# Four layers in one Trainium2 kernel: second cross-attention's norm and blocks, the scan's opening, and the order of the head loop in self-attention

## The chip, the cores and the metric

One core of one Trainium2 chip runs the whole program. The metric is the device time of one execution in microseconds; lower is better. Everything is float32. The engines are TensorE (PE in the profile, PEld its weight loads), VectorE (DVE), ScalarE (ACT), GpSimd (POOL) and SyncE (SP), which issues the transfers here. Each engine runs its own instructions in order, and they meet through semaphores.

## The reference

Four layers follow each other on `x` of 8 batches x 512 tokens x 256 features, with a context of 8 x 64 x 192.

```
L0: h = ln(x); x += Wo softmax(q k / sqrt(64)) v     16 heads of 64, 512 keys (self-attention)
    h = ln(x); x += attention(h, context)             16 heads of 64, 64 keys
    h = ln(x); x += (a * gelu(gate)) W2 + b2
L1: p = silu(context pre_w1) pre_w2; h = [p, x]       64 + 512 = 576 tokens in each batch
    4 layers: xz = rmsnorm(h) W_in; xi = silu(conv(x part)); dt, B, C = xi W_x
              state = exp(dt A) * state + dt * B * xi; y = (C . state + D xi) * silu(z); h += y W_out
    h = rmsnorm(h), the first 64 tokens dropped
L2: xn = layernorm(x); q = xn Wq; k, v = layernorm(context) Wkv; 16 heads of 16, 64 keys
    x += softmax(q k / 4) v Wproj + bproj             (second cross-attention)
    x += gelu(layernorm(x) W1 + b1) W2 + b2
L3: x += single-head attention of layernorm(x) over layernorm(context)
```

## The kernel before

`X` holds the activations in SBUF for the whole run, features on the partitions. The stages run one after the other, each in a block with one program for each engine, and a block ends when all its engines have ended: self-attention, first cross-attention, feed-forward, the scan (`mamba`), the last norm of L1, second cross-attention, feed-forward, last attention. All orders are written by hand. Banks 6 and 7 of PSUM are two lanes, `lane_v` (taken over mostly by VectorE) and `lane_s` (by ScalarE), each with a semaphore for full and one for free; events on a lane have a fixed order, so a step on a lane waits until the event before it has been read.

**Self-attention** (`self_attention`). A loop over 8 batches. Projections of q and k come first, 128x512 each. Then 18 iterations h: the program's heads go in 16 steps h, each with two units u. A unit of *scores* (L394) is the product of 128 queries with 512 keys for two heads (j), which go to banks 2u and 2u+1. VectorE takes the negated maximum of both (L456), ScalarE the two exponentials with their sums (L535), VectorE the reciprocal (L462), and GpSimd multiplies (L574). Two iterations later (LAG = 2, g = h - 2) a *turn* of 8 transposes (L385) lays the unit's probabilities out in banks 4 (copied by VectorE, L451) and 5 (by ScalarE, L527). A *mix* (L371) multiplies the values with both turned units of step g - 1, into a lane. Two mixes fill a lane, which VectorE (L470) or ScalarE (L507) copies to `q`. Between the units of every iteration TensorE's order is turn(g, 0), scores(h, 0), mix(g - 1), turn(g, 1), scores(h, 1). In the iterations h = 0 and 1 the values are projected (L339). While a batch runs, the next batch's norm is worked in: mean after g = 3, square after g = 4, variance after g = 9, scaling on VectorE after g = 10 (L480), and four key projections after g = 14. A unit of scores waits for the exponentials of the unit before it in the same banks, a turn for the multiplied probabilities and for the copies of the turn before it, a mix for both copies of its two turns.

**The scan** (`mamba`). 9 chunks of 512 columns in each of 4 layers, 36 bodies in a loop. A body has 32 pairs j: SyncE spreads dt and u over the partitions (`spread_dt`, `spread_u`, 4 transfers each, for 8 pairs) and loads B and C (`load_bc`, 16 transfers of 256 KB, each for one of 8 values a and one half q; `bc_ready[a // 2]` counts them); GpSimd multiplies u with B into a ring of 6 pairs (L2523), ScalarE makes exp(dt A) (L2492), VectorE scans (L2445) and multiplies with C (L2247) or GpSimd does (L2528), TensorE folds each pair into y (L2388) and works in the projections of the chunks ahead. The *opening* ahead of the loop does for the first chunk what the loop does one chunk ahead: norm, projections (L1956, L1974), silu, softplus, `times_x` (L2261, L2264: u = dt * xi for half of the channels and the reset of dt at a batch's begin), the spreads (L2276, L2283) and B and C (L2292). All engines of the opening but VectorE first wait for `set_up`, six small VectorE steps, one of which clears z (L2400, 128x4096). SyncE waits for all four counts of `u_done` ahead of the first spread; the spreads and then all 16 `load_bc` follow. The first matmul of the loop's count `summed` reads z (L2362).

**Second cross-attention** (`cross_attention_2`). 8 batches of 4 tiles (t) of 128 queries; n counts tiles. The keys of a batch lie as a block-diagonal matrix in `kblk`, the values in `vblk`, two buffers each, brought by `bring_blocks` in 8 + 2 transfers on one semaphore (L1199, L1203). For each tile: scores (L1364), VectorE maximum (L1406) and subtraction (L1410), ScalarE exponential (L1467), VectorE row sum (L1415) and reciprocal (L1417) one tile later, GpSimd multiplication (L1292), a turn two tiles later (L1346) and ScalarE's copy (L1479). Around it, per batch: mean of batch b + 2 (L1301, at t = 1), centring on VectorE (L1392, last but the residual in the iteration t = 1), square, variance of batch b + 1 (L1308, at t = 0), scale on GpSimd (L1285, after the multiplication of tile t = 0), the affine step on ScalarE (`affine`, L1442, at t = 2 ahead of the turned copy), queries (L1315, L1319, at t = 3), mix of batch b - 1 (L1326, L1330, at t = 2), and two output projections (L1339) with residuals on VectorE (L1398). Both output projections go over `lane_v`. SyncE brings the blocks of batch b when the mix of batch b - 2 has been read.

## Time and profile before

| | us |
|---|---|
| median of 3 runs | 6905.54 |
| lowest, highest | 6900.05, 6907.67 |
| the profiled execution's own time | 6903.88 |
| its span | 6902.1 |

| engine | busy us | share of the span |
|---|---|---|
| TensorE | 6161.2 | 89% |
| VectorE | 5114.1 | 74% |
| ScalarE | 3778.9 | 55% |
| GpSimd | 4645.8 | 67% |

The granted clock of TensorE is 0.947 of full over the profiled execution. The shares are means over stages with different limits, so each edit is read in its own stage: by the windows of the stages, then by the timeline in them. In a timeline row the first number is the start, the second the time from the start to the end of the group, then engine, line and operation, the operands, the count, and in brackets how long the engine was idle before and what released it. The ends of matmuls are modelled, so the distance from one start to the next is the safer number. A score matmul or a mix matmul of the program stands as two records.

### The profile page before, as it was taken

To read this page: it belongs to the slowest core of one execution; us is meant where nothing else is said; L and a number is where in the kernel's file an instruction comes from. 1 tells how busy PE (TensorE), PEld (TensorE's weight loads), DVE (VectorE), ACT (ScalarE), POOL (GpSimd) and SP (SyncE) were. 2 spreads that over 40 slices of the span, in tenths; PEclk is the share of its full clock that TensorE was granted. 3 is DMA by queue.
4 is the path that set the end of the run, shared out by engine and by line. 5 is a ranking of instruction groups with operands and counts; after the bars stand their busy time and mean duration, and the time that the engine had idled before them with its cause. 6 is when DMAs were issued, how large, how long until landed. Compare 5 with 4: busy or idle time off the path is not lost. (4 is left out here: it accounts for less than half of the span.)

```text
span 6902.1 us, 73695 instructions
## 1 busy us (share of the span) xinstructions
PE 6161.2 (89%) x20586; PEld 2565.1 (37%) x20586; DVE 5114.1 (74%) x5939; ACT 3778.9 (55%) x6915; POOL 4645.8 (67%) x2163
## 2 busy tenths in 40 slices
PE   9999999999998888888888888888888888888898
PEld 4444444544443333223333323333323333323444
DVE  4444444553226999999999999999999999995623
ACT  4444444532225666666666666666666666664432
POOL 3333333323006999999999999999999999993300
PEclk9999999999999999999999999999999999999998
DMA  2000000113003333333332333233333232332000
GB/s 77 0 0 0 0 0 0 63 44 105 12 0 71 74 78 74 77 90 79 73 80 69 80 84 84 68 80 68 80 84 84 68 85 64 86 78 56 5 0 25
DMA packets 228700, 387.51 MB, mean 56 GB/s; under 512 B 46304, under 2 KB 64416, under 8 KB 225936
## 3 DMA queue, kind: packets, MB, share of 16 engines
q1 hardware_dynamic: 228368, 383.75, 22.9%
q8 instruction: 127, 2.08, 0.1%
q14 instruction: 205, 1.68, 0.1%
HBM read 207.14 MB, written 23.40 MB: 33 GB/s over the span
## 5 line engine op out<-in xcount | busy, mean ns | idle before, releaser
L2523 POOL TENSOR_TENSOR work<-work,weights 128x1024 f32<-128x1024 f32 x1152 | 2692.2, 2363 | 24.3 <-DMA weights<-mamba_bc 13.0
L2388 PE MATMUL banks<-work 128*64 128x512 f32 x4608 | 1359.8, 672 | 568.2 <-POOL work L2528 568.0
L2445 DVE TENSOR_TENSOR_SCAN banks<-banks,work 128x512 f32<-128x512 f32 x1368 | 1712.4, 1274 | 39.5 <-ACT banks L2492 39.3
L2492 ACT ACTIVATE banks<-work 128x512 f32<-128x512 f32 x2304 | 1501.1, 680 | 68.6 <-DVE work L2241 43.2
L2445 DVE TENSOR_TENSOR_SCAN work<-banks,work 128x512 f32<-128x512 f32 x936 | 1175.1, 1271 | 109.2 <-ACT banks L2492 71.9
L2528 POOL TENSOR_TENSOR work<-work,weights 128x1024 f32<-128x1024 f32 x468 | 1103.9, 2359 | 159.7 <-ACT work L2118 159.7
L1956 PE MATMUL banks<-work,weights 128*128 128x512 f32 (+31 forms) x3796 | 1141.1, 451 | 3.0 <-DVE work L2214 3.0
L574 POOL TENSOR_TENSOR work<-work 128x1024 f32<-128x1024 f32 x256 | 484.4, 1895 | 802.6 <-DVE work L462 802.6
L2247 DVE TENSOR_TENSOR work<-banks,weights 128x512 f32<-128x512 f32 x1368 | 905.4, 673 | 0.0
L1956 PEld LDWEIGHTS banks<-work,weights 128*128 128x128 f32 x3796 | 634.4, 190 | 601.0 <-issue 523.5
L2388 PEld LDWEIGHTS banks<-work 128*64 128x64 f32 x4608 | 269.0, 144 | 1426.0 <-POOL work L2528 866.1
L2122 ACT ACTIVATE work<-banks 128x2 f32<-128x2 f32 x684 | 117.3, 171 | 1019.6 <-DVE work L2247 1011.2
L456 DVE TENSOR_REDUCE work<-banks 128x2 f32<-128x1024 f32 x256 | 312.3, 1223 | 155.6 <-PE banks L394 155.6
L535 ACT ACTIVATE work<-banks,work 128x512 f32<-128x512 f32 x512 | 346.5, 684 | 77.9 <-DVE work L456 77.9
L1974 PE MATMUL banks<-work,weights 128*128 128x512 f32 x592 | 351.9, 724 | 0.0
L1011 PE MATMUL banks<-work,weights 128*128 128x512 f32 x768 | 341.2, 598 | 9.7 <-ACT work L215 9.7
L451 DVE COPY work<-banks 128x512 f32<-128x512 f32 x256 | 175.2, 684 | 164.9 <-PE banks L385 164.9
L394 PE MATMUL banks<-work 64*128 64x512 f32 x1024 | 284.7, 638 | 5.6 <-ACT work L502 5.6
L385 PE MATMUL banks<-ident,work 128*128 128x128 f32 x2048 | 281.1, 279 | 5.1 <-ACT work L527 4.7
L527 ACT ACTIVATE work<-banks 128x512 f32<-128x512 f32 x256 | 152.8, 597 | 232.3 <-PE banks L385 231.8
L385 PEld LDWEIGHTS banks<-ident,work 128*128 128x128 f32 x2048 | 221.3, 140 | 150.8 <-issue 79.8
L371 PE MATMUL banks<-work 128*64 128x256 f32 x2048 | 249.3, 385 | 14.7 <-DVE work L480 8.4
(317 smaller groups left out, 7355.4 us busy)
## 6 DMA issues: line engine op xcount, KB each, us to landing
weights<-mamba_bc SPq DMA_DIRECT2D x592, 256.0 KB, 5.0
work<-work SPq DMA_DIRECT2D x1160, 128.0 KB, 2.3
weights<-mamba_taps SPq DMA_DIRECT2D x5, 2048.0 KB, 7.4
weights<-cross_vo SPq DMA_DIRECT2D x16, 512.0 KB, 6.9
mamba_taps<-work SPq DMA_DIRECT2D x4, 2048.0 KB, 6.7
cross_vo<-weights SPq DMA_DIRECT2D x6, 1024.0 KB, 9.0
work<-in_conv_rows SPq DMA_DIRECT2D x16, 256.0 KB, 7.1
out_T<-X SPq DMA_DIRECT2D x8, 512.0 KB, 3.3
```

The costliest lines, as they stand in the source:

```text
L385: mm = e.transpose(core.banks[:, 4 + j, kt * P:(kt + 1) * P], probs[:, 2 * (g % 2) + u, j, kt * P:(kt + 1) * P], core.ident[:])
L535: last = e.activation(probs[:, slot, j, :], core.banks[:, 2 * u + j, :], ACT.Exp, bias=nmax[:, slot, j:j + 1], accum_out=sums[:, slot, j:j ...
L574: e.tensor_tensor(probs[:, slot], probs[:, slot], rsum[:, slot, :].unsqueeze(2).to_broadcast([P, 2, T]), ALU.mult) \
L1011: mm = e.matmul(bank(i), w1[:, k, m * P:(m + 1) * P], normed[:, k, :], start=(k == 0), stop=(k == KD - 1))
L1956: mm = e.matmul(lane[:, a:b], conv_w[j][:, k, m * P:(m + 1) * P], nb[:, k, a + j:b + j], start=(d == 0 and k == 0), stop=(j == 0 and b == ...
L1974: mm = e.matmul(lane, z_w[:, k, m * P:(m + 1) * P], nb[:, k, TAPS - 1:], start=(k == 0), stop=(k == KD - 1))
L2247: last = e.tensor_tensor(ring_pair(n, j)[:, h, :], banks[:, slot_of(i), :], bc[:, j % SP_, 1, :], ALU.mult)
L2388: mm = e.matmul(ybank[k % 2][64 * h:64 * h + 64, :], fold, ring_pair(n, j)[:, h, :], start=False, stop=(a == SP_ - 1))
L2445: e.tensor_tensor_scan(ub if by_pool(j) else da, da, ub, state[:, i:i + 1], ALU.mult, ALU.add).then_inc(scanned, 1)
L2492: e.activation(banks[:, slot_of(i), :], dt_rep[:, k % 2, h, :], ACT.Exp, scale=decay[:, f:f + 1]).then_inc(da_full, 1)
L2523: e.tensor_tensor(ring_pair(n, j), u_rep[:, k % 2], bc[:, a, 0, :].unsqueeze(1).to_broadcast([P, 2, TC]), ALU.mult) \
L2528: e.tensor_tensor(ring_pair(n, q), ring_pair(n, q), bc[:, q % SP_, 1, :].unsqueeze(1).to_broadcast([P, 2, TC]), ALU.mult) \
```

## The change

Self-attention: TensorE's order in an iteration becomes turn(g, 0), scores(h, 0), scores(h, 1), turn(g, 1), mix(g - 1). VectorE's becomes copy of turn(g, 0), maximum of both units with the reciprocal of the step before between them, copy of turn(g, 1), reciprocal; the take-overs of mixed lanes (`V_TAKES`) come one iteration later, near its front, as do ScalarE's. ScalarE's order becomes copy, exponentials, copy, exponentials.

Second cross-attention: GpSimd scales batch b + 1 ahead of the multiplication of tile t = 0; ScalarE's affine step comes at t = 1 behind the turned copy; centring comes ahead of the row sum; the blocks' transfers are split into keys, issued when all scores of batch b - 2 are done, and values, issued as before, each with semaphores of its own; the mix waits for the values. The very last output projection goes over `lane_s`.

The scan: z is cleared on GpSimd, outside `set_up` (now 5 steps); ScalarE's silu of z waits for it in the opening; TensorE waits for a silu ahead of the matmul that reads z; SyncE issues four of the `load_bc` ahead of everything, then waits for the first half's `u_done` and not for both, spreads, and issues the other twelve; ScalarE waits for the last softplus step ahead of the loop.

```diff
-    KEYS_AHEAD, KEYS_HEAD, VALUES_AT = 4, H0 - 2, (0, 1)
+    KEYS_AHEAD, KEYS_HEAD, VALUES_AT, V_TAKES = 4, H0 - 2, (0, 1), {3: 0, 7: 2, 11: 4, 14: 6}
...
+                    if g >= 0:
+                        turn(g, 0)
+                    if h < H0:
+                        scores(h, 0)
+                        scores(h, 1)
+                    if g >= 0:
+                        turn(g, 1)
+                    if g >= 1:
+                        mix(g - 1)
...
+                    if g >= 0:
+                        take_turned(g, 0)
+                    if g in V_TAKES and g < 14:
+                        take_v(g)
+                    if h < H0:
+                        maximum(h, 0)
+                    if 0 < h <= H0:
+                        reciprocal(h - 1, 1)
+                    if h < H0:
+                        maximum(h, 1)
+                    if g >= 0:
+                        take_turned(g, 1)
+                    if h < H0:
+                        reciprocal(h, 0)
...
-                    if g >= 0 and g % 4 == 2:
-                        e.wait_ge(ln.v_full, V(1))
-                        e.tensor_copy(q[:, g // 2 - 1, :], core.lane_v).then_inc(ln.v_free, 1)
-                        V.add()
+                    if g == 14:
+                        take_v(g)
...
+                        take_turned(g, 0)
+                    if g >= 5 and g % 4 == 1:
+                        take_mixed((g - 1) // 2 - 1)
...
+                        exponential(h, 0)
+                    if g >= 0:
+                        take_turned(g, 1)
+                    if h < H0:
+                        exponential(h, 1)
...
-                    if g >= 4 and g % 4 == 0:
-                        take_mixed(g // 2 - 1)
...
+def bring_keys(e, two, b):
 
     for h in range(8):
         e.dma_start(two.kblk[HW2 * h:HW2 * h + HW2, b % 2, :, h * M:h * M + M],
-                    two.k_all[HW2 * h:HW2 * h + HW2, :, b * M:(b + 1) * M]).then_inc(two.blocks_in[b % 2], 16)
+                    two.k_all[HW2 * h:HW2 * h + HW2, :, b * M:(b + 1) * M]).then_inc(two.keys_in[b % 2], 16)
+
+
+def bring_values(e, two, b):
+
     for h in range(2):
         own, f = slice(h * M, h * M + M), h * HW2
         e.dma_start(two.vblk[own, b % 2, :, f:f + HW2], two.v_heads[b % 2 * M:b % 2 * M + M, b // 2, :, f:f + HW2]) \
-            .then_inc(two.blocks_in[b % 2], 16)
+            .then_inc(two.values_in[b % 2], 16)
...
-            bring_blocks(e, two, 0)
-            bring_blocks(e, two, 1)
+            for b in range(2):
+                bring_keys(e, two, b)
+                bring_values(e, two, b)
             load_weights(e, core, 0, [(2048, core.dram["L2_xattn_W1"]), (4096, core.dram["L2_xattn_W2"])])
             for b in range(2, B):
+                e.wait_ge(s_full, (b - 1) * QT)
+                bring_keys(e, two, b)
                 v_lane_read(e, ("mix", b - 2))
                 s_lane_read(e, ("mix", b - 2))
-                bring_blocks(e, two, b)
+                bring_values(e, two, b)
 
...
+                if b + 1 < B and t == 0:
+                    scale(b + 1)
                 view = groups(probs[:, t, :])
                 e.wait_ge(rsum_ready, n + 1)
                 e.tensor_tensor(view, view, rowsum[:, t, :].unsqueeze(2).to_broadcast([P, heads, M]), ALU.mult).then_inc(p_ready, 1)
-                if b + 1 < B and t == 0:
-                    scale(b + 1)
...
+                e.wait_ge(two.values_in[b % 2], VALUES_IN * (b // 2 + 1))
...
+                if (m, b) == (1, B - 1):
+                    s_lane_free(e, ("out1", b))
+                    for k in range(tiles):
+                        mm = e.matmul(lane_s, wo[:, k, P:D], mixed[:, k, :], start=(k == 0), stop=(k == tiles - 1))
+                    mm.then_inc(ln.s_full, 1)
+                    return
...
+                if b + 2 < B and t == 1:
+                    centre(b + 2)
                 if 1 <= n <= TILES:
                     s = (n - 1) % QT
                     e.wait_ge(exp_done, n)
...
                     e.reciprocal(rowsum[:, s, :], rowsum[:, s, :]).then_inc(rsum_ready, 1)
                 if b >= 2 and t == 0:
                     residual(b - 2, 1)
-                if b + 2 < B and t == 1:
-                    centre(b + 2)
...
-            residual(B - 1, 1)
+            s_lane_full(e, ("out1", B - 1))
+            x = core.X[:, 1, B - 1, PRE:S1]
+            e.scalar_tensor_tensor(out=x, in0=lane_s, scalar=core.v("bproj", 1), in1=x, op0=ALU.add, op1=ALU.add).then_inc(ln.s_free, 1)
...
-                if b + 1 < B and t == 2:
-                    affine(b + 1)
                 if b + 1 < B and t == 3:
                     take_query(b + 1)
                 if n >= BEHIND_T:
...
                     e.wait_ge(t_full, n - BEHIND_T + 1)
                     e.activation(probsT[:, :, s * P:(s + 1) * P], banks[:, 4:6, :].rearrange("p a (c q) -> p (a c) q", c=4), ACT.Copy) \
                         .then_inc(t_free, 1)
+                if b + 1 < B and t == 1:
+                    affine(b + 1)
...
+            else:
+                e.wait_ge(cleared, 1)
             e.activation(zn, zn, ACT.Silu).then_inc(silu, 1)
...
-            e.wait_ge(u_done, KI)
+            for a in range(2):
+                for q in range(2):
+                    load_bc(e, (0, -1), a, q, 0)
+            e.wait_ge(u_done, u_done_at((0, -1), 0, 2))
             spread_dt(e, 0)
             spread_u(e, 0)
-            for a in range(SP_):
+            for a in range(2, SP_):
                 for q in range(2):
                     load_bc(e, (0, -1), a, q, 0)
+            e.wait_ge(u_done, KI)
...
+            e.wait_ge(silu, 1)
             e.matmul(ybank[1], core.ident[:], z[:, 1, 0, :], start=True, stop=True).then_inc(summed, 1)
...
-            e.memset(z, 0.0).then_inc(set_up, 1)
...
+            e.wait_ge(soft, soft_at((0, -1), KI - 1, 3))
             with e.Fori(0, LAYERS // 2) as l:
...
+            e.memset(z, 0.0).then_inc(cleared, 1)
             e.wait_ge(set_up, SET_UP)
```

## Rows read from the trace of the kernel before

**Rows 1.** Windows by stage: start:end, length, busy us of PE, PEld, DVE, ACT, POOL; clock.

```profile
49.10:1307.00 1257.90, 1218.06 (x6133) 625.00 (x6132) 603.50 (x931) 591.61 (x1443) 484.37 (x256) 1.00 0.00 0
2043.20:2142.80 99.60, 79.13 (x199) 35.34 (x198) 25.00 (x42) 41.25 (x62) 18.11 (x13) 0.88 0.24 53
2142.80:6271.50 4128.70, 3565.01 (x10575) 1299.01 (x10575) 3963.83 (x4314) 2662.21 (x4780) 3929.31 (x1768) 0.93 0.33 78
6323.20:6552.10 228.90, 191.06 (x704) 89.63 (x704) 141.99 (x160) 109.85 (x137) 79.55 (x40) 0.99 0.06 14
```

**Rows 2.** Timeline of PE in self-attention, one iteration of the first batch.

```profile
121.00 1.09 PE L385 MATMUL banks<-ident,work 128*128 128x128 f32 x8
122.03 1.13 PE L394 MATMUL banks<-work 64*128 64x512 f32 x4
123.09 1.09 PE L385 MATMUL banks<-ident,work 128*128 128x128 f32 x8
...
125.18 1.95 PE L371 MATMUL banks<-work 128*64 128x256 f32 x16
127.06 1.09 PE L385 MATMUL banks<-ident,work 128*128 128x128 f32 x8
```

**Rows 3.** Timeline of PE: two units of scores without a step between, iteration 0.

```profile
50.41 1.99 PE L394 MATMUL banks<-work 64*128 64x512 f32 x8 [0.69 <-ACT work L502]
```

**Rows 4.** Timeline of PE: the two waits of a batch for the next batch's norm.

```profile
103.27 0.66 PE L385 MATMUL banks<-ident,work 128*128 128x128 f32 x4 [0.26 <-ACT work L527]
...
140.32 1.95 PE L371 MATMUL banks<-work 128*64 128x256 f32 x16 [1.20 <-DVE work L480]
```

**Rows 5.** Timeline of DVE and ACT in the iteration of rows 2.

```profile
123.20 1.23 DVE L456 TENSOR_REDUCE work<-banks 128x2 f32<-128x1024 f32 x1 [0.81 <-PE banks L394]
...
124.46 0.69 ACT L535 ACTIVATE work<-banks,work 128x512 f32<-128x512 f32 x1 [0.39 <-DVE work L456]
...
126.28 0.60 ACT L527 ACTIVATE work<-banks 128x512 f32<-128x512 f32 x1
...
127.75 0.69 DVE L451 COPY work<-banks 128x512 f32<-128x512 f32 x1 [1.16 <-PE banks L385]
```

**Rows 6.** Timeline of second cross-attention, around batch 5 and at its end.

```profile
6477.83 1.01 ACT L1479 ACTIVATE work<-banks 128x1024 f32<-128x1024 f32 x1
...
6478.16 1.22 DVE L1392 TENSOR_TENSOR work<-X,banks 128x512 f32<-128x512 f32 x2
...
6479.53 1.06 PE L1326 MATMUL banks<-work 128*32 128x512 f32 x8 [0.98 <-DVE work L1392]
...
6485.36 1.98 PE L1315 MATMUL banks<-work,weights 128*128 128x512 f32 x4 [1.17 <-ACT work L1442]
...
6492.18 1.95 PE L1364 MATMUL banks<-work 128*128 128x512 f32 x4 [0.53 <-DMA work<-work]
...
6549.07 1.98 PE L1339 MATMUL banks<-work,weights 128*128 128x512 f32 x4 [0.84 <-DVE X L1398]
```

**Rows 7.** Timeline of the scan's opening and first pairs, and a memset on POOL.

```profile
2045.31 3.47 DVE L2400 MEMSET work<- 128x4096 f32 x1 [0.80 <-issue]
...
2111.98 0.20 POOL L2264 TENSOR_TENSOR work<-work,one 128x2 f32<-128x2 f32 x1
...
2118.21 2.43 SPq L2276 DMA_DIRECT2D work<-work  x4
...
2125.04 0.17 ACT L2122 ACTIVATE work<-banks 128x2 f32<-128x2 f32 x1 [6.93 <-DMA work<-work]
...
2131.13 9.26 POOL L2523 TENSOR_TENSOR work<-work,weights 128x1024 f32<-128x1024 f32 x4 [13.00 <-DMA weights<-mamba_bc]
...
2142.76 1.98 PE L2388 MATMUL banks<-work 128*64 128x512 f32 x4 [6.99 <-POOL work L2528]
...
2150.07 1.08 PE L2388 MATMUL banks<-work 128*64 128x512 f32 x4
...
6271.45 1.80 POOL L2561 MEMSET work<- 128x2048 f32 x1 [22.75 <-POOLq L101]
```

115 lines of the change are left out of this document (56 added, 59 removed).

## The prediction

> **What bounds the kernel now.** I read the windows by stage first, because the change touches three stages with different limits [rows 1]. In self-attention TensorE is busy 1218.06 of 1257.90 us at full clock; the other engines are at half or less. In the scan loop, which is 4128.7 us and holds no edited instruction, VectorE (3963.83) and GpSimd (3929.31) are near full. The opening before it is a chain of short steps. In the second cross-attention TensorE is busy 191.06 of 228.90 us. So in the first stage the question is TensorE's own rate, in the other two it is its gaps. I then read TensorE's timeline of one head pair [rows 2, 3], the gaps in it [rows 4], the work of the engines that feed it [rows 5], and the gaps of the other two stages [rows 6, 7].
>
> **Part 1, self-attention.** No instruction is added or removed. Per iteration TensorE now does turn, scores, mix, turn, scores; after it does turn, scores, scores, turn, mix. From start to start a turn of 8 transposes takes 1.03 us, a score unit 1.06, a mix 1.88 [rows 2]: 1.03 + 1.06 + 1.03 + 1.06 + 1.88 = 6.06. The three use different shapes of the array (128x128, 64x128, 128x64), and the first instruction after a change of shape is late. Two units of scores in a row have one such change less: 8 score matmuls are busy 1.99 us [rows 3] where 4 are busy 1.13, and since that end is modelled about 0.07 to 0.08 us past the next start (1.13 against 1.06), two units hold the engine 1.91 instead of 2.12. That is 0.21 us per iteration. A turn that goes straight into a mix has no row in this group; I take the 1.03 of a turn that goes into scores, since both leave the transposes' shape, and bound it by 0.1 either way. The iterations with both scores and mix are 13 per batch: 2.7 us.
>
> The order of the copies must not take this back. Laid out from the start of the first scores at 0: the maximum starts at 1.17 and takes 1.23, the two exponentials follow to about 3.9 (two of 0.69 and the read of the sum), ScalarE's copy of the second turn ends at 4.4, the second exponentials at 5.8; VectorE's second maximum ends near 3.6 and its copy of the second turn at 4.4 [rows 5]. The next iteration begins its first turn at 4.82 and needs the copies (0.4 spare), its first scores at 5.85 need the first exponentials (1.9 spare), its second scores at 6.8 need the second (1.0 spare). So TensorE stays the bound. The tightest point is 0.4 us.
>
> Two gaps per batch exist only while the next batch's norm runs. The mix of pair 10 waits 1.20 us for norm's scaling on VectorE, and a turn waits 0.26 us for a ScalarE copy queued behind the square; with the restart they cost 1.27 and 0.5 [rows 4]. After the change the mix stands a turn and a score unit later, and a mix lies between the delayed copy and the next turn: I cost both at nothing, which gives 1.8 in 7 of 8 batches. One gap is new: in the first iteration with a turn there is no mix behind the second turn, so the next turn waits for VectorE's copy, which stands behind two maxima: 1.17 + 1.23 + 1.2 + 0.69 = 4.3, plus a turn's 0.87, makes 5.2 from scores to scores where two turns and two score units, 4.18, passed before: 1.0 lost. At the end of a batch the paired turns wait for each other's copies and the last mix no longer does; I take 0.3 gained, and 0.5 in the last batch, which projects no keys there. Sum: 7 x (2.7 + 1.8 - 1.0 + 0.3) + (2.7 - 1.0 + 0.5) = 28.8; I take **28**, bounds 20 and 33.
>
> **Part 2, the scan's opening.** VectorE's memset of 3.47 us stands ahead of the semaphore on which ScalarE, TensorE and GpSimd all start. It moves to GpSimd, where a memset of half the size takes 1.80, so about 3.6; GpSimd's next needed step is the product in the trace at about 2110, so this is covered. If it were not, the loss would be the same 3.6. Gain: 3.4 on the whole chain.
>
> Then SyncE no longer waits for both products of dt and x, but for the first pair, which is done at 2112.18 instead of the 2118.21 of the first spreading transfer; and 4 of the 16 transfers of B and C are issued ahead of the 8 spreads instead of behind them [rows 7]. GpSimd's first multiplication of the loop sat 13.00 us until 2131.13 for them. Now it can start when the spreads land, 6.8 us (2125.04 - 2118.21) after 2112.2 - 3.4 = 2108.8, so at 2115.6, and the third pair, whose transfers land behind the spreads, near 2121.6. These 12 transfers move at the rate they moved before, and each pair of them is there before GpSimd asks, but for that third one (1.3 us). What is late next is TensorE: it ends the opening at 2142.76 - 6.99 = 2135.77, so now at 2132.3, and from there it runs without a gap, as in every body. It gains the 3.4, the 6.99 of idle time, and the half-rate start after it (4 matmuls took 1.98 us, and take 1.08 once the clock is back [rows 7]; two such groups, 1.6): 12.0. ScalarE waits for TensorE's last z block in its first pairs, and by my layout it and VectorE come out about 11 us sooner. I take **11.7**; bounds: 3.4, if the loop's first wait only moves, and 14. The added waits (TensorE for the first silu, ScalarE for the last softplus step) are met some microseconds before the waiting engine arrives, with only the loop queued behind them: nothing.
>
> **Part 3, second cross-attention.** Per batch TensorE has three gaps: 0.98 ahead of the mix, for VectorE's centring; 1.17 ahead of the queries, for norm's last step; 0.53 ahead of a batch's first scores, for the transfers of the blocks [rows 6]. The idle figure starts 0.16 us after the next matmul could have (4 matmuls are busy 1.88 and take 1.72), and a restart costs up to 0.1, so they cost 1.14, 1.4 and 0.75. Scale on GpSimd and the last step on ScalarE now come about a tile sooner (some 5 us), the key blocks a batch sooner: the second and the third gap go. Both steps are put ahead of work that was not urgent: GpSimd was free before the next product, and the ScalarE slot follows a copy. SyncE waits for the scores ahead of the keys and for the mix ahead of the values only; behind it is queued the next batch alone.
>
> The first gap is not simply gone. Centring moves ahead of the row sum, so the lane is free 1.2 us sooner, but the mix also needs ScalarE's copy of the fourth tile, which ends at 6477.83 + 1.01 = 6478.84 where TensorE would arrive at 6478.4: 0.45 stays. And the row sum is 1.22 us later, GpSimd's product with it, and the turn behind the mix waits about 0.7 for that, since TensorE now arrives sooner. Net per batch: 1.14 + 1.4 + 0.75 - 0.45 - 0.7 = 2.1; six times 12.6. The first batch, without a mix, loses about 0.2 to the later row sum. The last projection goes to the other lane and no longer waits for VectorE [rows 6]: 1.1. Together **13.5**, bounds 6 and 17.
>
> **The sum.** 28 + 11.7 + 13.5 = 53.2. The profiled execution has a span of 6902.1 and took 6903.88; the median of the runs shown is 1.7 above that. So 6905.54 - 53.2 = **6852**.
>
> **The rivals.** (a) **The copies become the bound of self-attention.** The 0.4 us spare ahead of each batch's turns is the smallest in the plan. If ScalarE's copy behind the first exponentials came 0.6 late, the head would again take 6.06 and only parts 2 and 3 and the lost gaps stay: 13 x 8 x 0.21 = 22 less, 6874. Against it: each duration of the plan is a row. (b) **The scan's opening keeps only the memset's 3.4**, because the spreads and the loads share the transfer engines and the loop's first pairs meet the old times: 8.3 less, 6860. For it: GpSimd's 13.00 of waiting was on transfers. Against it: 4 of them now go out while nothing else moves. (c) **The memset on GpSimd holds VectorE off**, so that the common start comes no sooner: 2.7 to 3.4 less, 6855. Nothing in the trace has a GpSimd memset beside the small VectorE steps. The Trainium skill, "SBUF — State Buffer", Who interferes with whom, says that the two engines share a port pair, and that whoever starts first keeps it for the whole instruction and the other fully blocks, in some modes of VectorE; by that rule VectorE's fold and memsets would end when GpSimd's memset does. The same section says that a VectorE step with two inputs is not held by a GpSimd step that only writes, which would leave the sum as it is. (d) **Slower.** The loop's 4128.7 us depend on how VectorE, GpSimd and TensorE fall against each other, and it is now entered in another phase: GpSimd some 13 us ahead, TensorE 12. If each of the 36 bodies kept a longer rhythm, the gains are eaten at 53.2 / 36 = 1.5 us per body; at 1.9 the kernel takes 6920. Against it: the ring of six pairs lets GpSimd be ahead only so far, and the first body was in the same rhythm as the others although it was entered with TensorE idle. (e) **The reordering does less than planned in more than one place**, new waits of 0.1 to 0.2 us in every head and every tile, so that half of parts 1 and 3 is left: 6873.
>
> **Chances.** Forecast 0.62 (its own range 6845 to 6860), (a) 0.08, (b) 0.10, (c) 0.08, (d) 0.04, (e) 0.08. The range takes the forecast, (b), (c) and the bounds of the terms nearest to it: **6842 to 6868**. A measurement of this kernel can tell about 0.2% (14 us) from no change. All cases but (d) and a wide miss in (e) are faster by more: faster 0.93, same 0.03, slower 0.04.
>
> **What would show it.** In the changed trace: two score units at 1.91 us and 5.85 from one first turn to the next; no wait for norm's scaling ahead of a mix in self-attention, and one new wait in each batch's first turned head; the common start of the opening 3.4 us sooner after the stage's beginning; GpSimd's first loop multiplication some 15 us sooner against the stage's start, and TensorE's first fold without 6.99 of idle time; the loop's length unchanged within 3 us; no wait for a transfer or for norm's last step in the second cross-attention, and a new short wait of the turn behind the mix for GpSimd. The prediction is wrong if the head stays at 6.06, if the loop's length changes, or if the turn behind the mix loses what the queries gain.

## The result, and the profile after

The changed kernel takes **6856.25 us** (median; 6855.31 to 6856.48), where the kernel before took 6905.54: 49.3 less, where 53 was forecast. The ratio is 0.993, with a 95% interval of 0.9918 to 0.9942, wholly below 1: the change makes the kernel 0.7% faster. The profiled execution took 6856.39 with a span of 6854.6, so the spans differ by 47.5.

Windows of the kernel after, for the stages of [rows 1]; the columns are those of that group (the second window holds the scan's opening and its loop).

```profile
48.00:1280.00 1232.00, 1190.83 (x6134) 633.61 (x6133) 594.22 (x932) 587.90 (x1443) 480.00 (x256) 1.00 0.00 0
2017.70:6230.00 4212.30, 3646.39 (x10770) 1335.25 (x10770) 3984.16 (x4353) 2703.66 (x4840) 3951.07 (x1780) 0.93 0.33 77
6281.80:6503.30 221.50, 193.70 (x704) 91.72 (x704) 142.03 (x160) 109.11 (x137) 79.47 (x40) 0.96 0.06 15
```

In the second cross-attention TensorE is busy 193.70 us where [rows 1] has 191.06, with a matmul count that did not change, and the granted clock fell from 0.99 to 0.96. That is the first sign of what went wrong in the sum. The next table has, for this kernel and for all that follow, the length of each stretch in the profiled execution (us, from the first and last instructions of the stages in the trace; "to scan" is the first cross-attention with its feed-forward, "scan" goes from its first instruction to the final norm's).

| kernel | self-att. ends | to scan | scan | final norm | cross-att. 2 | feed-fwd. 2 | last stage | span |
|---|---|---|---|---|---|---|---|---|
| before | 1310.5 | 733.8 | 4227.1 | 51.8 | 228.9 | 265.3 | 84.7 | 6902.1 |
| after | 1283.6 | 734.2 | 4212.7 | 51.4 | 221.4 | 266.7 | 84.6 | 6854.6 |
| centre_back | 1283.8 | 733.4 | 4213.9 | 51.8 | 215.3 | 266.8 | 77.6 | 6842.6 |
| scale_affine_back | 1285.1 | 735.2 | 4214.5 | 50.1 | 226.2 | 265.5 | 84.6 | 6861.2 |
| keys_back | 1284.9 | 733.6 | 4215.0 | 50.1 | 221.5 | 268.2 | 78.3 | 6851.7 |
| blocks_together | 1285.2 | 733.7 | 4215.1 | 50.1 | 231.6 | 268.3 | 78.2 | 6862.1 |
| last_on_v | 1283.9 | 735.5 | 4216.4 | 51.8 | 219.8 | 266.7 | 78.1 | 6852.0 |
| scores_apart | 1306.2 | 733.6 | 4214.2 | 51.8 | 218.7 | 265.2 | 84.6 | 6874.2 |
| memset_back | 1284.8 | 735.5 | 4213.7 | 50.1 | 222.1 | 268.2 | 78.5 | 6853.0 |
| loads_back | 1285.3 | 733.2 | 4224.0 | 51.8 | 218.7 | 265.2 | 84.6 | 6862.7 |
| mean_sooner | 1284.8 | 733.9 | 4215.2 | 50.1 | 212.2 | 266.8 | 77.5 | 6840.5 |
| delay_after | 1285.3 | 735.3 | 4214.4 | 51.8 | 218.6 | 266.8 | 86.1 | 6858.2 |
| delay_best | 1285.3 | 734.5 | 4212.7 | 51.4 | 213.4 | 266.6 | 81.8 | 6845.6 |

Read down a column first. A stage that was not edited differs from row to row: the last stage is 77.5 to 78.5 or 84.6, and the changed second cross-attention is 218.6 to 222.1 in the five kernels that share its code (after, scores_apart, memset_back, loads_back, delay_after). A single profile therefore prices an edit in that stage only to about 3 us by the stage's length, and one in the last stage only to 7; the terms have to be read from steps. Each row is one profiled execution, so whether a length belongs to the kernel or to the execution is not shown.

**Self-attention**, timeline of PE: a turn of the first iteration that has one, and a later iteration:

```profile
73.10 1.07 PE L382 MATMUL banks<-ident,work 128*128 128x128 f32 x8 [1.33 <-DVE work L456]
...
109.88 1.09 PE L382 MATMUL banks<-ident,work 128*128 128x128 f32 x8
110.90 1.99 PE L392 MATMUL banks<-work 64*128 64x512 f32 x8
112.82 1.09 PE L382 MATMUL banks<-ident,work 128*128 128x128 f32 x8
113.84 1.95 PE L371 MATMUL banks<-work 128*64 128x256 f32 x16
115.72 1.09 PE L382 MATMUL banks<-ident,work 128*128 128x128 f32 x8
```

Two score units hold TensorE from 110.90 to 112.82, 1.92; from first turn to first turn are 5.84, where [rows 2] has 6.06. The second turn is followed by the mix after 1.02, no dearer than into scores. A batch takes 158.30 from its first scores to the next one's, and took 161.77. Neither wait of [rows 4] is left. The new one is the 1.33 of the first iteration with a turn, which now takes 5.33 instead of 4.20.

**The opening**, timeline of all engines, POOL's memset and what ran beside it; then GpSimd's first steps of the loop and TensorE's first fold:

```profile
2017.76 3.51 POOL L2560 MEMSET work<- 128x4096 f32 x1 [315.24 <-POOLq L999]
...
2017.85 0.11 DVE L2455 MEMSET work<- 128x64 f32 x1 [0.37 <-PEq L999]
...
2018.14 0.06 DVE L2462 MEMSET work<- 128x1 f32 x1
...
2019.06 0.20 ACT L2521 ACTIVATE work<-work 128x1 f32<-128x1 f32 x1
...
2088.48 4.65 POOL L2580 TENSOR_TENSOR work<-work,weights 128x1024 f32<-128x1024 f32 x2 [1.94 <-DMA work<-work]
2094.19 4.68 POOL L2580 TENSOR_TENSOR work<-work,weights 128x1024 f32<-128x1024 f32 x2 [1.06 <-DMA weights<-mamba_bc]
...
2103.36 1.94 PE L2444 MATMUL banks<-work 128*64 128x512 f32 x8
```

The memset runs on GpSimd from 2017.76 to 2021.27, and VectorE's short steps beside it take 0.06 each as they did without it: nothing holds VectorE off, so rival (c) did not come. GpSimd's first multiplication is 70.7 us behind the stage's start (2017.8), where in [rows 7] it was 86.8 behind 2044.3. The first fold has no idle time, where [rows 7] shows 6.99.

**The second cross-attention**, timeline of PE: in the first batch; around the mix of a steady batch; and at the end.

```profile
6316.68 1.34 PE L1393 MATMUL banks<-ident,work 128*128 128x128 f32 x8 [3.73 <-POOL work L1334]
6317.81 3.37 PE L1411 MATMUL banks<-work 128*128 128x512 f32 x4
...
6360.83 1.07 PE L1367 MATMUL banks<-work 128*32 128x512 f32 x8 [0.34 <-ACT work L1526]
6361.72 1.04 PE L1371 MATMUL banks<-work 128*32 128x512 f32 x8
6363.42 1.09 PE L1393 MATMUL banks<-ident,work 128*128 128x128 f32 x8 [0.67 <-POOL work L1334]
...
6494.50 1.62 PE L1367 MATMUL banks<-work 128*32 128x512 f32 x8 [1.11 <-ACT work L1526]
...
6500.35 1.88 PE L1381 MATMUL banks<-work,weights 128*128 128x512 f32 x4
```

In the steady batch (24.06 us, before 25.85) the three gaps of [rows 6] have become two: 0.34 ahead of the mix, now for ScalarE's copy, and the forecast new one of the turn behind it, 0.67 for GpSimd. The queries and the scores wait for nothing. The last projection stands on the other lane without a gap. But in the first batch the first turn waits 3.73, and the scores behind it take 3.37 for four matmuls that take 1.88 elsewhere: that is the lower of TensorE's two clocks (1.2 and 2.4 GHz; the granted clock is 0.50 from 6317.4 to 6320.8). So is the mix at 6494.50 (1.62 against 1.07).

### The profile page after: what moved, and what is told of

It is laid out like the page before. It is cut to its first block and busy times, and to the rows that moved or that the text cites. A ratio compares the mean times of both kernels' runs of the same rounds, so it can differ in the third digit from the quotient of the medians.

```text
span 6854.6 us, 73694 instructions
## 1 busy us (share of the span) xinstructions
PE 6140.2 (90%) x20586; PEld 2577.3 (38%) x20586; DVE 5100.9 (74%) x5938; ACT 3774.8 (55%) x6915; POOL 4645.0 (68%) x2164
## 3 DMA queue, kind: packets, MB, share of 16 engines
HBM read 207.14 MB, written 23.40 MB: 34 GB/s over the span
## 5 line engine op out<-in xcount | busy, mean ns | idle before, releaser
L1043 PE MATMUL banks<-work,weights 128*128 128x512 f32 x768 | 340.7, 598 | 10.6 <-ACT work L215 10.6
L2023 PE MATMUL banks<-work,weights 128*128 128x512 f32 x592 | 350.1, 721 | 0.0
L382 PE MATMUL banks<-ident,work 128*128 128x128 f32 x2048 | 278.0, 279 | 17.7 <-DVE work L456 14.1
L382 PEld LDWEIGHTS banks<-ident,work 128*128 128x128 f32 x2048 | 221.4, 141 | 158.7 <-issue 118.0
L392 PE MATMUL banks<-work 64*128 64x512 f32 x1024 | 254.4, 615 | 5.6 <-ACT work L527 5.6
L330 PE MATMUL banks<-work,weights 128*128 128x512 f32 x512 | 226.1, 600 | 16.7 <-DVE X L511 6.7
```

The lines of the kernel that those rows point to most:

```text
L382: mm = e.transpose(core.banks[:, 4 + j, kt * P:(kt + 1) * P], probs[:, 2 * (g % 2) + u, j, kt * P:(kt + 1) * P], core.ident[:])
L1043: mm = e.matmul(bank(i), w1[:, k, m * P:(m + 1) * P], normed[:, k, :], start=(k == 0), stop=(k == KD - 1))
L2023: mm = e.matmul(lane, z_w[:, k, m * P:(m + 1) * P], nb[:, k, TAPS - 1:], start=(k == 0), stop=(k == KD - 1))
```

## The experiments

Each is the changed kernel with the edit shown; delay_best has mean_sooner's edit too. Only mean_sooner and delay_after were run four times, the others once. The kernel before, run seven times beside some of them, took 6896.47 to 6909.00 us, so one total says little below some 10 us, and the edits are priced by the steps of the profiled execution.

**1. centre_back: the centring behind the row sum again.** Only the order on VectorE.

```diff
-                if b + 2 < B and t == 1:
-                    centre(b + 2)
                 if 1 <= n <= TILES:
...
                 if b >= 2 and t == 0:
                     residual(b - 2, 1)
+                if b + 2 < B and t == 1:
+                    centre(b + 2)
```

> The changed kernel, with the centring of the batch after next put back behind the row sum and its reciprocal on VectorE. The second cross-attention of the changed kernel lasts 221.4 us. Theory 1, this placement is where most of the missing gain went: the 0.73 us that the turn behind the mix waits for GpSimd's product goes, and with it about 1.2 us of the wait ahead of the first turn of the stage; the period of a batch goes from 24.06 to about 23.7, the first batch from 22.7 to 21.6, and the stage lasts 218 to 219.5 us. Theory 2, the turn would wait in any order, because TensorE now arrives sooner, and the missing gain went to stretches at TensorE's lower clock: 221.4 within 0.7.

It took 6844.37 us, the stage 215.3: shorter than either theory had it. Timeline of PE in centre_back, first batch and a steady one:

```profile
6315.14 1.09 PE L1393 MATMUL banks<-ident,work 128*128 128x128 f32 x8 [2.54 <-POOL work L1334]
6316.07 1.88 PE L1411 MATMUL banks<-work 128*128 128x512 f32 x4
...
6358.15 1.07 PE L1367 MATMUL banks<-work 128*32 128x512 f32 x8 [0.97 <-DVE work L1439]
6359.01 1.07 PE L1371 MATMUL banks<-work 128*32 128x512 f32 x8
6360.00 1.09 PE L1393 MATMUL banks<-ident,work 128*128 128x128 f32 x8
```

In the steady batch the order is a wash: 0.97 for VectorE comes back ahead of the mix, and 0.34 + 0.67 go; period 23.96 against 24.06. The first turn waits 1.19 less (2.54 against 3.73), as theory 1 has it, and the scores behind it run at the higher clock (1.88 against 3.37). The first batch takes 19.86 instead of 22.74: 1.2 of wait, and 1.7 that the lower clock behind the longer wait had cost (the turn 1.34 and the scores 3.37, against 1.09 and 1.88). Of the other 3.2 of the 6.1, 1.4 is the lower clock at the stage's start (19.9 to the first scores against 21.3) and 1.3 in the tail, neither of which the edit touched, and 0.5 came in the six batches behind the first. Both theories held a part.

**2. scale_affine_back: norm's scaling and last step late again.**

```diff
-                if b + 1 < B and t == 0:
-                    scale(b + 1)
                 view = groups(probs[:, t, :])
                 ... ALU.mult).then_inc(p_ready, 1)
+                if b + 1 < B and t == 0:
+                    scale(b + 1)
```
and ScalarE's `affine(b + 1)` from behind the copy of tile 1 back to ahead of the copy of tile 2.

> The changed kernel, with norm's scaling put back behind the product of a batch's first tile on GpSimd and norm's last step put back into the third tile on ScalarE. Theory 1, these two moves are what ended the wait of the queries (1.17 us, 1.4 with the restart): the wait is back, the period is about 25.3 instead of 24.06, and the stage lasts 228 to 230 instead of 221.4. Theory 2, the wait for the transfers was what set the period and the scaling was beside it: the period rises by under 0.4 and the stage lasts under 224.

The period is 25.16, the stage 226.2, the time 6862.98. Theory 1: the wait of [rows 6] is back, here in a steady batch, and the rest did not move. The two moves were put back together, so how they share it is not shown. The stage came out 2 under the forecast: the tail ran at the higher clock (1.3 less), and the period rose by 1.1 where 1.25 was expected.

```profile
6390.15 1.06 PE L1367 MATMUL banks<-work 128*32 128x512 f32 x8 [0.34 <-ACT work L1528]
...
6396.62 1.99 PE L1355 MATMUL banks<-work,weights 128*128 128x512 f32 x4 [1.07 <-ACT work L1491]
```

**3. keys_back: the key blocks issued behind the mix again, with their own semaphore kept.**

```diff
-                e.wait_ge(s_full, (b - 1) * QT)
-                bring_keys(e, two, b)
                 v_lane_read(e, ("mix", b - 2))
                 s_lane_read(e, ("mix", b - 2))
+                bring_keys(e, two, b)
                 bring_values(e, two, b)
```

> The changed kernel, with the transfers of a batch's key blocks again issued behind the mix of the batch two before, ahead of the value blocks. Theory 1, as the prediction costed it, each gap by itself: only the 0.53 us wait ahead of a batch's first scores is back (0.75 with the restart), period 24.8, stage 226. Theory 2, the transfers take as long as they did from the mix to their landing, so that what the queries gained turns into a longer wait for them, 0.53 + 1.4 - 0.3 or more: period 25.5 to 26.2, stage 230 to 234, no sooner than before the change.

Neither: one batch of 25.06, the steady ones 24.2, the stage 221.5. With the waits split, issuing the keys sooner is worth 0.15 to 0.2 us in most batches and 1.0 in one, 0.3 on average over six. So what had ended the wait for transfers?

**4. blocks_together: as keys_back, and the scores wait for all ten transfers.**

```diff
                         e.wait_ge(two.keys_in[b % 2], KEYS_IN * (b // 2 + 1))
+                        e.wait_ge(two.values_in[b % 2], VALUES_IN * (b // 2 + 1))
```

> As keys_back (the eight key transfers of a batch issued behind the mix of the batch two before, ahead of the two value transfers), and a batch's first scores wait for all ten again, as before the change. In keys_back the keys of the fifth batch landed at 6398.97 us and its values at 6400.55, 1.6 later, and its steady batch took 24.2 us, one 25.06. Theory 1, the split of the wait is what the change lives on and the sooner issue is worth only 0.2: the scores wait for the values, period 25.7 to 25.9, no shorter than before the change, and the stage lasts 228 to 232 us, 9 to 10 longer than keys_back if the lower clock falls as there. Theory 2, the ten transfers land in time once norm's steps are early, or the wait only moves beside another: period under 24.8, stage under 225.

Theory 1, on its numbers: batches of 25.83 to 25.86, the stage 231.6, the time 6863.92. Timeline of PE at a batch's first scores, in keys_back (the one batch that waits) and in blocks_together:

```profile
6374.96 1.96 PE L1410 MATMUL banks<-work 128*128 128x512 f32 x4 [0.77 <-DMA work<-work]
```

```profile
6377.69 1.95 PE L1411 MATMUL banks<-work 128*128 128x512 f32 x4 [1.57 <-DMA work<-work]
...
6390.32 1.07 PE L1366 MATMUL banks<-work 128*32 128x512 f32 x8 [0.34 <-ACT work L1526]
...
6403.52 1.96 PE L1411 MATMUL banks<-work 128*128 128x512 f32 x4 [1.54 <-DMA work<-work]
```

This kernel has the early scaling and last step, and no wait of the queries. Its batch still takes the 25.85 of the kernel before. The way from a batch's scores through the mix and the transfers issued behind it to the next batch's scores is a ring. SyncE's rows show its second half, in the kernel before and in blocks_together (the scores come at 6492.18 and 6403.52), and the values in the kernel after:

```profile
6483.99 5.11 SPq L1199 DMA_DIRECT2D work<-work  x8
```

```profile
6395.42 5.11 SPq L1232 DMA_DIRECT2D work<-work  x8
```

```profile
6389.99 1.32 SPq L1240 DMA_DIRECT2D work<-work  x2
```

From the issue to the scores it takes 8.19 and 8.10, and from a batch's first scores to the issue 17.7 in both. The queries' wait of [rows 6], at 6485.36, lies inside the 8.19: ending it only lets TensorE arrive sooner at the end of the ring, where the time comes back as waiting (0.53 in [rows 6], 1.57 here). Here it was the separate wait for the keys that shortened the ring, by 1.6. The sooner issue without the separate wait was not run, and it may open the ring as well: two values alone, issued at 6389.99 as in the kernel after, would land near 6392.9 by an estimate from these rows (1.3 to issue, and the 1.6 from the end of the issue to the scores here), 3.5 ahead of the next scores at 6396.4.

**5. last_on_v: the last projection on VectorE's lane again.** `project_out(B - 1, 1)` goes to `lane_v`, and the last residual reads it there.

> The changed kernel, with the last projection of the stage again on VectorE's lane, behind the residual of the one before. Theory 1, as predicted, the other lane saves 1.1 us: the stretch from the last batch's first scores to the end of the stage goes from 35.4 to about 36.5. Theory 2, it saves nothing here, since the tail did not get shorter with it (35.2 before the change, 35.4 after): 35.4 within 0.3, and the difference lies in the stretch of lower clock beside it.

From the last batch's first scores to the stage's end it takes 35.2 us, against 34.1 where the other lane is used and the clock stays high (scores_apart, loads_back), and 35.4 in the kernel after. So the lane saves its 1.1, and in the kernel after the lower clock took 1.4 (from the last mix to the first half of the last projection 4.06, in loads_back 2.69). Theory 1 is right on the price, theory 2 on where it went. The wait it removes, in last_on_v:

```profile
6504.24 1.98 PE L1380 MATMUL banks<-work,weights 128*128 128x512 f32 x4 [0.84 <-DVE X L1439]
```

**6. scores_apart: the two score units apart, the mix still last.**

```diff
                     if h < H0:
                         scores(h, 0)
-                        scores(h, 1)
                     if g >= 0:
                         turn(g, 1)
+                    if h < H0:
+                        scores(h, 1)
```
VectorE takes the second turn ahead of the second maximum, ScalarE ahead of the exponentials.

> The changed kernel, with the two score units of self-attention again apart: TensorE does turn, scores, turn, scores, mix, and the two other engines copy and reduce in that order. Against the changed kernel this is one more change of the array's shape per iteration; the mix is still last. Theory 1, the gain in self-attention is that change of shape, 0.21 us each: the iteration takes 6.02 to 6.10 instead of 5.84, and self-attention ends 18 to 25 us later than at 1283.6. Theory 2, the gain is from the mix's new place behind both turns, which ended waits: the iteration stays under 5.9 and the stage ends within 5 us of 1283.6.

It took 6875.98; self-attention ends at 1306.2, 22.6 later, the batch takes 160.97 against 158.30. Timeline of PE:

```profile
112.72 1.09 PE L382 MATMUL banks<-ident,work 128*128 128x128 f32 x8
113.74 1.13 PE L392 MATMUL banks<-work 64*128 64x512 f32 x4
114.80 1.09 PE L382 MATMUL banks<-ident,work 128*128 128x128 f32 x8
115.82 1.13 PE L392 MATMUL banks<-work 64*128 64x512 f32 x4
116.88 1.95 PE L371 MATMUL banks<-work 128*64 128x256 f32 x16
118.76 1.09 PE L382 MATMUL banks<-ident,work 128*128 128x128 f32 x8
```

No wait, and 6.04 from turn to turn. Theory 1: 2.67 per batch over 13 iterations is 0.205 us for one seam less, a change of the array's shape, which the prediction had from two rows as 0.21. This is the larger part of self-attention's gain: 2.67 of the 3.47 us per batch. No run changes the shape and leaves all else. What speaks for the shape is a turn between matmuls of its own shape, in the second cross-attention of the kernel after, which takes 0.87 from start to start, where the turn above takes 1.02:

```profile
6353.43 1.04 PE L1393 MATMUL banks<-ident,work 128*128 128x128 f32 x8
6354.30 1.88 PE L1411 MATMUL banks<-work 128*128 128x512 f32 x4
```

**7. memset_back: the memset of z on VectorE.** `e.memset(z, 0.0)` stands behind `memset(state)` on VectorE again.

> The changed kernel, with the memset of the z buffer again on VectorE, in its old place ahead of the common start of the scan's opening. The stage from the scan's first instruction to the final norm lasts 4212.7 to 4216.4 us in the five runs that have the changed opening. Theory 1, the whole chain waits for it: ScalarE's and TensorE's first steps of the stage come 3.4 us later against its start, the first fold of the loop too, and the stage lasts 4216 to 4220. Theory 2, the weights, tables or the clock hide a part of it: the first steps come 3.4 later, but the first fold comes less than 2 us later.

ScalarE's first step comes 4.68 us behind the stage's start instead of 1.29, and up to the second mean's matmuls, at 42.8 us instead of 39.2 in the kernel after and 39.5 in centre_back, the distance holds. The stretch from there to the ident product ahead of the first fold, in memset_back and in centre_back, which has the changed opening (windows; the last columns are the granted clock, the DMA share and GB/s):

```profile
2063.10:2108.50 45.40, 41.93 (x123) 19.79 (x124) 19.03 (x24) 28.76 (x46) 18.15 (x10) 0.96 0.50 118
```

```profile
2056.70:2104.30 47.60, 44.78 (x123) 20.74 (x124) 19.03 (x24) 28.93 (x46) 18.69 (x10) 0.89 0.48 112
```

The same 123 matmuls keep TensorE busy 41.93 us at a granted clock of 0.96 and 44.78 at 0.89. So the first fold comes 89.1 us behind the start, only 1.0 later than in centre_back (88.0), though 3.5 later than in the kernel after (85.6), whose stretch also ran at 0.96. Against the kernel after theory 1 has the fold right, against centre_back theory 2. The memset is worth its 3.4 in steps. In the stage's length, 4213.7, it does not show at all: that lies inside the 3.7 by which the ten kernels with the changed opening differ.

**8. loads_back: SyncE's old opening order.** Both products are waited for, spread, and then all 16 loads of B and C are issued.

> The changed kernel, with SyncE's opening order as before: it waits for both products of dt and x, spreads them, and then issues all 16 loads of B and C. Theory 1, this order held GpSimd and TensorE off and that cost stays to the end: GpSimd's first multiplication of the loop comes 12 to 14 us later against the stage's start, TensorE is idle for some 7 us before its first fold again, and the stage lasts 8 to 10 us longer, 4221 to 4226. Theory 2, the loop's ring takes the delay in: GpSimd's first multiplication is 13 later, but the stage lasts under 4218, inside or near what the runs with the changed opening show.

Theory 1. Timelines of POOL and PE in loads_back:

```profile
2102.35 9.25 POOL L2576 TENSOR_TENSOR work<-work,weights 128x1024 f32<-128x1024 f32 x4 [13.43 <-DMA weights<-mamba_bc]
...
2113.96 3.32 PE L2440 MATMUL banks<-work 128*64 128x512 f32 x8 [7.41 <-POOL work L2581]
```

GpSimd waits 13.43 again (13.00 in [rows 7]), TensorE 7.41, and the eight folds take 3.32 instead of 1.94. The first multiplication stands 83.9 us behind the start, where the kernels with the changed order have 71 to 74, and the stage lasts 4224.0, against 4214.4 as the mean of the ten kernels with the changed opening: 9.6. The time is 6864.53.

**9. mean_sooner: a version made from the above.** The centring behind the row sum, and from the second batch on the mean of the batch after next one tile sooner, the second half of the last projection one tile later.

```diff
-                    if b >= 2:
-                        project_out(b - 2, 1)
-                if b + 2 < B and t == 1:
+                if b + 2 < B and t == int(b == 0):
                     mean(b + 2)
+                if b >= 2 and t == 1:
+                    project_out(b - 2, 1)
```
VectorE's `centre` and `residual` follow in the same way behind the row sum, and the lane's order of events with them.

> The changed kernel, with centring behind the row sum as in centre_back, and from the second batch on the mean of the batch after next one tile sooner, ahead of the second half of the last projection, which moves to the next tile (centring and the residual follow it). Of centre_back's batch of 23.96 us TensorE waits 0.97 ahead of the mix for VectorE's centring. Theory 1, the short residual now stands where the centring stood, so that the mix waits only for ScalarE's copy of the fourth tile (0.34) and the turn behind it for nothing new: period 23.2 to 23.4, the stage 211 to 213 us against 215.3. Theory 2, the row sum behind it is what is late, in either order, and the wait moves on to the turn: period 23.8 to 24.0, stage 214 to 216. The total depends besides on how the lower clock falls in the last stage, which lasts 77.6 to 78.3 or 84.6 us: 6842 less 0 to 4, or 6849 less 0 to 4.

It took **6845.05 us** (6842.38 to 6846.30), ratio to the kernel before 0.9916, 95% interval 0.9899 to 0.9932. Timeline of PE, steady batch:

```profile
6360.02 1.06 PE L1367 MATMUL banks<-work 128*32 128x512 f32 x8 [0.42 <-ACT work L1526]
6360.88 1.07 PE L1371 MATMUL banks<-work 128*32 128x512 f32 x8
6361.88 1.09 PE L1393 MATMUL banks<-ident,work 128*128 128x128 f32 x8
```

Theory 1: one wait of 0.42 is left, the period is 23.40, the stage 212.2. Against the kernel after the spans differ by 14.1, of which the cross-attention gives 9.2 (some 2.6 of that is the lower clock at its start and end) and the last stage, unedited, 7.1; the scan is 2.5 longer in this profile, which is of the fastest of the four runs. The medians differ by 11.2. A gain over centre_back (6844.37, one run) is shown in the period alone, 23.40 against 23.96, and not in the total.

**10, 11. delay_after and delay_best: what decides the last stage.** A memset of 2048 columns on VectorE, for which TensorE's first matmul of the last stage waits, in the kernel after and in mean_sooner.

> The changed kernel with one instruction more, a memset of 2048 columns on VectorE (about 1.75 us by the 3.47 of the 4096-column one) at the start of the last stage, for which TensorE's first matmul of that stage waits. The last stage, in which nothing was edited so far, lasts 84.6 us in before, after, scale_affine_back, scores_apart and loads_back, and 77.5 to 78.5 in centre_back, keys_back, last_on_v, memset_back and mean_sooner. Theory 1, that is only the place at which TensorE's lower clock falls, and it hangs on the moment of entry: entered 1.8 us later, the stage of the changed kernel falls into the short form, about 79.5 with the delay in it, and the kernel is some 5 us faster for an added instruction: 6851. Theory 2, something before it, left behind by the earlier stages, decides: the stage lasts 86.4 and the kernel takes 6858.

> mean_sooner with the same delay ahead of the last stage, which lasts 77.5 us in it. Theory 1, the moment of entry decides: entered 1.8 us later it falls into the long form, 86.4 with the delay, and the kernel takes about 6851 to 6854 (8.9 more). Theory 2, the earlier stages decide: 79.3, the kernel 1.8 us longer than mean_sooner, 6844 to 6848.

delay_after took 6860.49 (6860.08 to 6864.17; ratio to the kernel before 0.9942, 0.9926 to 0.9959), delay_best 6847.44. The last stage, counted from the memset, takes 86.1 and 81.8, in windows of delay_after and delay_best:

```profile
6772.10:6858.20 86.10, 65.35 (x272) 42.90 (x272) 39.80 (x53) 16.32 (x25) 11.21 (x8) 0.70 0.13 49
```

```profile
6763.80:6845.60 81.80, 62.15 (x272) 39.19 (x272) 39.87 (x53) 16.33 (x25) 11.22 (x8) 0.73 0.14 52
```

Timeline of PE at the entry, in delay_after and in the kernel after:

```profile
6774.43 5.40 PE L1602 MATMUL banks<-X,mean_d 128*128 128x512 f32 x8 [3.40 <-DVE work L1652]
```

```profile
6769.98 3.67 PE L1601 MATMUL banks<-X,mean_d 128*128 128x512 f32 x8 [1.11 <-PEq L999]
```

Theory 1 missed in both: it had 79.5 and 86.4. Theory 2 had 86.4 and 79.3, so it was right on the first within 0.3 and 2.5 short on the second, where the total, 6847.44, lies inside its 6844 to 6848. But the delay was no neutral shift: the idle time rose from 1.11 to 3.40, 2.3 and not 1.8, and the eight matmuls behind it took 1.7 longer, in both kernels. That is 4.0 of the 4.3 by which the stage grew in mean_sooner's kernel; in the kernel after the stage grew by only 1.5, and TensorE's busy time, 65.35, is that without the delay (65.47). So the runs speak against the moment of entry as what decides between the two forms, and for something before it, without showing what. The last stage in the kernel after and in centre_back, windows:

```profile
6770.00:6854.60 84.60, 65.47 (x272) 44.25 (x272) 38.06 (x52) 16.27 (x25) 11.24 (x8) 0.69 0.13 50
```

```profile
6765.00:6842.60 77.60, 59.89 (x272) 38.64 (x272) 37.99 (x52) 16.30 (x25) 11.22 (x8) 0.74 0.15 55
```

The same instructions with the same work on the other engines: TensorE is busy 65.47 at a mean granted clock of 0.69, and 59.89 at 0.74. Its busy time accounts for 5.6 of the 7.0. Why the one execution falls into the one form and another into the other stays open.

## Why the prediction was right or wrong

The time was 6856.25, 4 us above the forecast and inside its range, with the sign right. By the profiled spans 47.5 were gained where 53.2 were forecast: 26.9, 14.4 and 7.5 in the three parts for 28, 11.7 and 13.5, and 1.3 lost outside them, nearly all of it in the unedited feed-forward behind the cross-attention. That the total came so near is in part luck: where the lower clock fell, beyond the 1.6 us that the sum has for it, added 2.4 to the second part and took 4.3 from the third.

**Self-attention, 26.9 for 28.** Each step held, and nearly in size. Iteration 5.84 (forecast 5.85), seam 0.205 (0.21), both waits for norm gone. The first iteration with a turn lost 1.13 (1.0), the end of a batch gained about 0.16 (0.3), which is what is left over: 3.47 - 2.67 - 1.77 + 1.13, with the two waits for norm at the forecast's 1.27 and 0.5. Seven batches give 24.3, the last one 2.1 (forecast 2.2), and 0.5 came ahead of the first scores. Rival (a), the copies as the bound, did not come: the plan's 0.4 us of room was there. That the seam between the score units is the cause is shown by scores_apart.

**The opening, 14.4 for 11.7.** The step that was mis-sized is the clock. The prediction granted it 1.6 us, at the folds; the kernel after gained about 2.4 more ahead of them, because its stretch ran at 0.96 and not at the 0.89 of centre_back. Over the ten profiles with the changed opening the stage lasts 4212.7 to 4216.4, mean 4214.4, so that the change is worth 12.7 on average, near the 11.7. The common start came 3.39 sooner (forecast 3.4), and loads_back prices the order at 9.6 (the forecast's 11.7 - 3.4 is 8.3). That the stage keeps the memset's 3.4 is not shown as firmly: the kernel before and loads_back, which differ in the scan by it and by the added waits, are 3.1 apart (4227.1 and 4224.0), but memset_back's stage is no longer than the ten. GpSimd's first multiplication came 16.1 sooner (forecast some 15), TensorE was not idle (forecast), and the loop's own rhythm did not change, so that neither (b), nor (c), nor (d) came. VectorE's fold and its small memsets, which (c) saw held, took 0.22 and 0.06 us beside GpSimd's memset, as without it.

**The second cross-attention, 7.5 for 13.5.** This is the part whose sum failed. Three things, by the steps of the prediction.
- The clock, which the sum had at nothing: 1.2 at the stage's start, 1.4 in the tail, and 1.7 in the first batch, 4.3 together. The first two come and go from kernel to kernel (the stage is 218.7 in scores_apart and loads_back, so 10.2 gained). The third is the change's own: it is in all nine kernels with the centring ahead of the row sum, where the first turn waits 3.73 (first batch 22.7 long), and in none of the three without (2.54, 19.9), nor in the kernel before (2.54). The step "the first batch loses about 0.2" had the wait right (22.74 - 1.7 - 20.84 = 0.2) and not what a longer idle time does to the clock behind it.
- The steady batch gained 1.8 and not 2.1, the six batches together 10.7 and not 12.6 (from the first scores of one to those of the next: 2.1, four times 1.8, 1.3). The waits of the mix and the turn were forecast as 0.45 and 0.7 and cost 0.50 and 0.73 with their restarts, and out0 begins 0.17 later behind its turn. The tail's 1.1 held (last_on_v). Without the clock the part is worth 10.7 - 0.2 + 1.1 = 11.6.
- The reasons were right only in part. The centring, costed as a gain of 0.7 against a loss of 0.7, is indeed worth nothing in a steady batch (24.06 against 23.96), and over the stage it loses 3.4 (215.3 in centre_back, 218.7 in scores_apart). The transfers' 0.75 was read as a gap of its own. blocks_together shows that it was the end of a ring: with the ten transfers issued and waited for together, the 1.4 of the queries brings nothing. Adding up the gaps of one trace came near here only because the change opened the ring as well. The part of it that the prediction named, the keys a batch sooner, is worth 0.3 per batch once the waits are split, and was not run alone.

Rival (e), half of parts 1 and 3, came for part 3 in size, but not by its mechanism of new small waits.

## What to carry to other kernels

Gaps on one engine add up only if they are not ends of the same ring: before a removed wait is counted, follow each remaining one back to its start and ask whether its distance is fixed. A transfer that is waited for with others that are needed later deserves a semaphore of its own: here that gave 1.6 us per batch, and the sooner issue on top of it 0.3. And where TensorE can be at either clock, price a wait by what it does to the matmuls behind it as well, and an edit by its steps rather than by one profile's stage length, since unedited stages moved by up to 7 us from one kernel's profile to another's.

## What the runs showed of the hardware

- **The lower clock is worth more than the small waits.** An idle time of 3.73 us ahead of the first turn was followed by a stretch at the lower clock in all nine kernels that have it (four score matmuls in 3.37 us in the kernel after), one of 2.54 in none of four (1.88). The idle time just ahead is not all: behind the same 1.11 us the last mix took 1.62 in the kernel after and 1.07 in loads_back. In the last stage the delay raised the idle time from 1.11 to 3.40, and eight matmuls took 5.40 instead of 3.67. The Trainium skill, "TensorE: Matmul & The Clock Gate", Part 1, says that the engine is at the lower rate by default and that activity releases it, and that how many slow matmuls a kernel shows at its start varies from run to run. The two levels agree with the rows. Here the totals of the kernel after lie within 1.2 us (6855.31 to 6856.48) and those of the kernel before within 12.5 (6896.47 to 6909.00), and stages with the same code differed by up to 7 us from profile to profile.
- **A seam where the array's shape changes costs 0.2 us** in this mix of 128x128, 64x128 and 128x64 matmuls: 160.97 against 158.30 us for 13 of them. A turn without such seams takes 0.87 us, one between them 1.02.
- **GpSimd's memset did not hold VectorE's small steps**: 0.06 us each for the memsets and 0.22 for the fold, beside it and without it. The Trainium skill, "SBUF — State Buffer", Who interferes with whom, has VectorE's steps blocked in some modes only, which it gives for copy, cast and tensor_scalar and not for the steps here, so (c) read it too widely; no run here shows those modes.
